# Second group of degree matmuls issued two units earlier in the first graph pass

## What is computed

```python
deg = jax.ops.segment_sum(jnp.ones_like(dst, dtype=x.dtype), dst, num_segments=n_nodes)
dinv = jnp.where(deg > 0, jax.lax.rsqrt(deg), 0.0)
norm = dinv[src] * dinv[dst]
```

## Time and profile before

| | |
|---|---|
| median of three executions | 1940.42 us |
| lowest and highest | 1938.17, 1953.45 us |
| the profiled execution | 1938.17 us |
| its span | 1936.4 us, 1.8 us less than its time |
| TensorE's mean granted clock | 0.973 of full speed |
| TensorE busy | 1739.8 us, 90% of the span |

### The profile page before, as it was taken

One profiled execution on the slowest core, in us unless ns is written; L12 is line 12 of the kernel. 1 busy time (PEld: TensorE's weight loads), 2 busy tenths in 40 slices (PEclk: granted clock), 3 DMA queues, 4 the chain that ended last, 5 costly groups with the idle time before them and its releaser, 6 DMA issues.

```text
span 1936.4 us, 30601 instructions
## 1 busy us (share of the span) xinstructions
PE 1739.8 (90%) x10210; PEld 1374.5 (71%) x10214; DVE 925.6 (48%) x1526; ACT 562.9 (29%) x843; POOL 153.3 (8%) x165
## 2 busy tenths in 40 slices
PE   1589999888788999999999999999999999988991
PEld 1278888888776677777777777766677777776781
DVE  5999999999883111111032233423213234335343
ACT  0013567788885000001011111433300000014440
POOL 3000000000000000000000000000000000141354
PEclk8789999999999999999999999999999999999996
DMA  3050334445557844445433334100064443443454
GB/s 91 1 172 22 127 141 175 191 190 211 212 212 303 246 136 138 141 143 153 153 119 119 118 118 131 56 1 0 17 219 128 136 120 117 135 148 101 153 160 136
DMA packets 125902, 260.94 MB, mean 135 GB/s; under 512 B 14924, under 2 KB 67302, under 8 KB 125466
## 3 DMA queue, kind: packets, MB, share of 16 engines
q1 hardware_dynamic: 108154, 240.30, 36.7%
q0 software_dynamic: 5568, 12.82, 2.2%
q10 hardware_dynamic: 12128, 7.16, 1.4%
HBM read 160.44 MB, written 108.04 MB: 139 GB/s over the span
## 4 chain that ended last, share of the span: by engine, by line
issue 54%; PE 28%; DVE 9%; ACT 4%; DMA 1%; POOL 1%; DVEq 1%; ACTq 0%; SPq 0%; POOLq 0%
PE ps L1814 10%; PE ps L1880 6%; DVE act_c L1246 3%; PE ps L1815 3%; PE ps L2100 3%; PE ps L2084 2%; ACT wide L754 2%; ACT ps L702 2%; PE ps L1785 1%; PE ps L1897 1%; POOL act_c L1060 1%; PE ps L2092 1%; PE ps L2076 1%; DMA wide<-in_edge_weight_dram 0%; DMA act_c<-expert_replies,pair_tab 0%
## 5 line engine op out<-in xcount | busy, mean ns | idle before, releaser
L1880 PE MATMUL ps<-wide 128*128 128x320 f32 (+1 forms) x2000 | 533.3, 427 | 0.0
L1814 PE MATMUL ps<-early,act_c 128*128 128x200 bf16 x3552 | 438.8, 252 | 61.2 <-DVE act_c L1246 30.7
L1880 PEld LDWEIGHTS ps<-wide 128*128 128x128 f32 x2000 | 378.2, 190 | 141.8 <-issue 0.8
L1814 PEld LDWEIGHTS ps<-early,act_c 128*128 128x128 bf16 x3552 | 327.2, 98 | 82.6 <-issue 80.9
L1815 PE MATMUL ps<-early,act_c 128*128 128x208 bf16 x1184 | 301.7, 255 | 0.0
L1246 DVE TENSOR_TENSOR act_c<-act_c,pair_tab 128x3072 bf16<-128x3072 bf16 x148 | 256.6, 1752 | 26.1 <-PE ps L1815 25.6
L1880 PE MATMUL ps<-wide,act_a 128*128 128x320 f32 (+1 forms) x1000 | 265.6, 428 | 3.4 <-DMA wide<-weight_matrix 3.4
L1880 PEld LDWEIGHTS ps<-wide,act_a 128*128 128x128 f32 x1000 | 190.7, 191 | 76.8 <-DMA wide<-weight_matrix 3.6
L754 ACT COPY wide<-ps 128x832 f32<-128x832 f32 x200 | 169.9, 849 | 106.5 <-PE ps L1815 104.5
L702 ACT ACTIVATE ps<-wide 128x832 f32 (+1 forms) x200 | 173.4, 868 | 35.0 <-ACT wide L754 33.6
L1350 DVE TENSOR_TENSOR wide<-ps,rows 128x1280 f32<-128x1280 f32 x10 | 14.9, 1492 | 318.3 <-PE ps L1897 318.3
(11 more groups left out here) (232 smaller groups left out, 1350.5 us busy)
## 6 DMA issues: line engine op xcount, KB each, us to landing
wide<-weight_matrix SPq DMA_DIRECT2D x90, 800.0 KB, 4.5
wide<-count_matrix SPq DMA_DIRECT2D x45, 800.0 KB, 4.5
weight_matrix<-wide SPq DMA_DIRECT2D x60, 480.0 KB, 2.5
count_matrix<-wide SPq DMA_DIRECT2D x60, 480.0 KB, 2.5
weight_matrix<-wide SPq DMA_DIRECT2D x20, 560.0 KB, 2.7
count_matrix<-wide SPq DMA_DIRECT2D x20, 560.0 KB, 2.7
expert_replies<-wide SPq DMA_DIRECT2D x63, 128.0 KB, 1.7
wide<-weight_matrix SPq DMA_DIRECT2D x20, 400.0 KB, 3.8
```

The lines of the kernel that those rows point to most:

```text
L1814: nc.tensor.matmul(weights, hot_parts[:, slot % MASK_BATCHES, part, two, :, k], hot_key[:, mask_slot, mask_two, 0:WCOLS, k], start=False, ...
L1880: i = nc.tensor.matmul(ps[:, 2 * sub + h, 0:n], features[:, q * QUADS + t, h * P:(h + 1) * P], moving, start=q == 0 and t == 0, stop=q == ...
```

## The change

`degrees(1)` stands behind unit (1, 1) in place of (1, 3).

```diff
-            beside = {(0, UNITS - 1): lambda: degrees(0), (1, 3): lambda: degrees(1)}
+            beside = {(0, UNITS - 1): lambda: degrees(0), (1, 1): lambda: degrees(1)}
```

## The result

| | before | changed |
|---|---|---|
| median of 14 executions | 1952.47 us | 1963.39 us |
| lowest and highest | 1937.5, 1957.15 | 1951.64, 1967.49 |
| span of the profiled execution | 1936.4 us | 1961.6 us |
| mean granted clock of TensorE in it | 0.973 | 0.962 |

The ratio is 1.0067, with a 95% interval of 1.0046 to 1.0089: slower by 9 to 17 us. The two medians differ by 10.9 us, against 11.15 us in the prediction. But the time itself, 1963.39 us, lies outside the range of 1945 to 1958 us, since the kernel before is not at 1940 us in the median but at 1952 us.

A forecast was written before the change was run, and what follows sets the result against it. The prediction took TensorE's instruction order, busy without a gap around the change, as the bound. Moved matmuls 0, wait 9.35 and slow clock 1.8 us summed to 11.15 us; on 1940.42 us that is 1951.6, predicted 1951, range 1945 to 1958 us.

The forecast's parts named there:

- The range: Whole kernel: the time would lie between 1945 and 1958 us, leaving out no more than 2 in 10.
- a median that may itself lie 2 us lower or higher: Base of the forecast time: the kernel before has a median of 1940.42 us, give or take 2 us.
- The wait: At the moved degree matmuls behind unit (1, 1): TensorE stalls for ScalarE's copy of part 0, 9.35 us (8.96 to 9.7).
- ScalarE is where it was: ScalarE's queue ahead of the degree wait: unchanged, still issuing weight loads, so it counts degrees_taken at 662.93 us.
- the hand-over: From the end of ScalarE's copy to the first degree matmul: 0.12 us plus 0.27 us of operand load, 0.39 us.
- The clock: TensorE's restart after the wait: granted clock 0.50 for a stretch, costing half its length, 1.8 us (1.45 to 2.7).
- The sum: Whole change: 0 for the moved matmuls, 9.35 us of wait and 1.8 us of slow clock make 11.15 us.
- Beside the path: After degrees(1): ScalarE's second copy, VectorE's two instructions and GpSimd's power come about 0.4 us later, at no cost.
- No cost: Rival at the degree wait: ScalarE finishes its loads by 651.15 us, so no stall, 1938 to 1941 us; chance 6%.
- The 50 ns: Sequencer dispatch per DMA: 35 loads take about 2 us, freeing ScalarE at 623 us; the prediction followed the trace's 39.0 us.
- Part is given back: Rival in later stages: a wait such as the last stage's 6.2 us absorbs delay, leaving 4.95 us, 1945.4 us; chance 5%.
- The restart is dearer: Rival after the wait: clock falls again or stays low for two longest stretches, 14.75 us in all, 1955.2 us; chance 8%.

The follow-up runs named there:

- after_again: The changed order, degree part 1 behind unit (1, 1), on before_again in place of the kernel before: 1970.85 us in the median.
- wide_bias_after: The changed order with the gate operands widened to 128 rows as in wide_bias: 1981.56 us, 0.9998 of before.
- wide_bias_after_2: wide_bias_after measured again, side by side with wide_bias_2 on the same chip: 1984.84 us.
- loads_behind: The changed order with the last 18 of ScalarE's 35 weight loads issued behind its copy of degree part 0: 1955.08 us, 1.0027 of before.
- wide_bias: before_again with the expert stage's gate operands (gate_t, out_bias, sel) widened from 5 to 128 partitions, the rest zeros: 1938.43 us, 0.9951 of before.
- before_again: The kernel before with one extra register operation each on ScalarE and TensorE for two first-stage waits; base of the experiments: 1956.57 us, 1.0039 of before.
- wide_bias_2: wide_bias measured again, beside slower executions of the kernel before: 1974.89 us.

## Why the prediction was right and wrong

**The range: wrong.** The step that failed is the base, "a median that may itself lie 2 us lower or higher": 1940.42 us, where fourteen executions give 1952.47 us, 12 us more. It took three executions for the level of the kernel, while a kernel on two levels some 14 us apart can show two low ones of three. I had the sign of it in hand, 1953.45 us, and took it for a stray value that moves the median by 3 us. The sum of 11.15 us on the median of fourteen would have given 1963.6 us.

**The wait: right in kind, too long.** Predicted 9.35 us, measured 5.65 us in the changed kernel and 7.54, 9.91 and 9.25 us in three executions of the same order. Three things made the difference in the first. TensorE arrived at 644.21 + 10.93 = 655.14 us, 1.2 us later, as the whole chain began later. ScalarE was done earlier, its copy starting at 658.75 us in place of 661.03 us, since the last two loads took 1.16 us in place of 3.42 us; "ScalarE is where it was" held the trace of one execution for a constant. And the hand-over cost 0.14 us, not 0.39 us: the first matmul starts at 660.79 us, 0.03 us behind the start of the load of its stationary operand (660.76 us), where the earlier trace rows have 0.27 us. The load itself did not run during the wait.

**The clock: right in kind, too short.** Predicted 1.8 us, bounds 1.45 and 2.7 us; measured 3.1 us in the changed kernel and 2.4 us in after_again. The stretch at 0.50 lasted 6 us, more than the longest of the three restarts in the earlier trace rows; in two more executions of this order the price was 1.5 and 2.8 us (wide_bias_after, wide_bias_after_2). The Trainium skill, "TensorE: Matmul & The Clock Gate", Part 1, is borne out as far as it goes: a wait brought the low clock and sustained work lifted it.

**The sum: right, with luck in the last digits.** 11.15 us predicted; 9.95 us between the kernels with wide operands, 10.9 us between the medians, 9 to 17 us by the interval of the ratio. In the profiled execution the wait was oversized by 3.7 us and the restart undersized by 1.3 us, and the change cost 8.9 us; in three others of this order it was 10.1, 11.6 and 12.2 us. That the medians differ by just 10.9 us is chance within that spread.

**Beside the path: right.** VectorE's step started at 666.26 us, 1.7 us before the 667.97 us of the kernel before, although its matmuls had been moved forward by two units; 0.4 us later was predicted, and ScalarE's earlier end makes the difference. No other wait of TensorE appeared.

**The rivals.** "No cost" fell with the 5.65 us. The 50 ns that the sentences behind it take from the Trainium skill, "DMA: Bandwidth & Descriptors", section "Anatomy of one DMA", stand there for DMAs that GpSimd issues, and these loads are ScalarE's; its 35 loads took 35.5 us in the changed kernel. "Part is given back" fell with wide_bias_after_2: 9.95 us reach the end. "The restart is dearer" came true by a part: 3.1 us, not 5.4.

## What to carry to other kernels

Where a step waits for an engine that works through its instructions in order, its place in the program is worth nothing before that engine's release; look at what stands in front of the release, and move that instead, as loads_behind did. A row of DMA issues on a computing engine is such an obstacle: here 35 of them, ahead of the copy, held ScalarE for 35.5 to 41 us. Before a forecast in absolute time, look at the spread of the executions, and where it has two heads, find what they differ in: here it was worth more than the change. And before a gain is put down to one cause, look for it in the trace: most of what wide_bias gained was at the full clock.

## What had not been expected of the hardware

TensorE's granted clock fell to 0.50 while the engine was busy for 14.97 of 15.00 us, and stayed there for 14 to 34 us, in a stage with matmuls of 5 rows. It did so in some executions and not in others, and each such stretch costs half its length. With the rows filled up with zeros to 128, and no other instruction of TensorE changed, the spread of twelve executions went from 20 us (before_again) to 4 us (wide_bias; 7 us in wide_bias_2), and no such stretch was seen. The Trainium skill, "TensorE: Matmul & The Clock Gate", section "HAM oscillation", warns of idle gaps only; here busy stretches were hit, and the measurement decides. Why the clock falls in one execution and not in the next was not found.

The second is that matmuls with operands of 5 rows cost more than those of 128 at the full clock: 135.5 us against 123.8 us for the same work of the expert stage (before against wide_bias, 543 and 542 matmul records). In the kernels with wide operands this is worth more than the slow stretches.

The third is how much ScalarE's release moves: counted from the start of `degrees(0)`, its copy of part 0 ended between 19.9 us (changed kernel) and 24.1 us (wide_bias_after) later in profiled executions, with the same loads and copies in front of it.
